# The first expert stage of an image network: experts, norms and q/k/v products of three images in one round

## The reference

```python
t = _to_tokens(x)                                   # per image: 4096 tokens of 128 channels
t = t + _L0_ffn_ref(_ln_t(t), ...)
x = _from_tokens(t, x)
... _L1_conv_ref(_ln_c(x), L1_conv_w_qkv, ...)      # begins with qkv = w_qkv (384 x 128) @ x

# inside _L0_ffn_ref: two of eight experts, the same two for all tokens of an image
h = gelu(einsum('nd,edf->enf', xf, W1) + b1)        # 128 -> 256
y = einsum('enf,efd->end', h, W2) + b2              # 256 -> 128
out = einsum('ne,end->nd', w_dense, y)
out = _layer_norm(out + x, gamma, beta)
```

## Time and profile before

| | |
|---|---|
| median of three runs | 3686.75 us |
| profiled execution | 3690.16 us, its span 3688.4 us |
| TensorE busy over the span | 3175.2 us (86%) |
| VectorE, ScalarE, GpSimd busy | 45%, 41%, 22% |
| mean granted TensorE clock | 0.906 of full speed |
| first expert stage, from its first `up` to its last product | 698.5 to 1476.2 us |

### The profile page before, as it was taken

How to read it: one execution, slowest core, us unless ns; L and a number is a source line. 1 busy time by engine, 2 the same in 40 slices (tenths; PEclk the granted TensorE clock), 3 DMA queues, 4 the chain that set the end, 5 groups by cost and what they waited for, 6 DMA issues and landing times. The chain is left out here.

```text
span 3688.4 us, 66878 instructions
## 1 busy us (share of the span) xinstructions
PE 3175.2 (86%) x27136; PEld 1709.4 (46%) x27136; DVE 1662.3 (45%) x2332; ACT 1520.3 (41%) x2263; POOL 810.5 (22%) x694
## 2 busy tenths in 40 slices
PE   5656675499989997799997779999999999999999
PEld 1146321344445453466665334646364545546444
DVE  5724256465555543111111254545454545545453
ACT  3311253266666664111213344545354444445433
POOL 2410242133333343111110112121211111121221
PEclk7768766699999997899999789999999999999999
DMA  5421464313333323777777321413222231313000
GB/s 187 151 75 23 136 241 207 141 46 137 137 137 137 137 92 143 197 213 215 209 211 250 116 79 46 132 52 103 75 92 91 65 99 54 114 41 126 12 12 24
DMA packets 192537, 438.59 MB, mean 119 GB/s; under 512 B 33340, under 2 KB 100156, under 8 KB 183740
## 3 DMA queue, kind: packets, MB, share of 16 engines
q1 hardware_dynamic: 192356, 436.20, 35.7%
HBM read 247.40 MB, written 188.75 MB: 118 GB/s over the span
## 5 line engine op out<-in xcount | busy, mean ns | idle before, releaser
L2115 DVE TENSOR_TENSOR d_hid_scaled<-d_hid_scaled,d_ps 128x512 f32<-128x512 f32 x512 | 331.1, 684 | 605.3 <-PE d_ps L1802 553.5
L1791 PE MATMUL d_ps<-d_hid_scaled,d_w 128*128 128x512 f32 x1024 | 526.2, 596 | 1.0 <-DVE d_hid_scaled L2115 1.0
L1976 ACT ACTIVATE d_hid_scaled<-d_ps,d_b 128x512 f32<-128x512 f32 x512 | 349.9, 686 | 381.3 <-PE d_ps L1780 368.0
L1519 PE MATMUL c_ps<-c_pad,c_weight 32*32 32x512 f32 x13824 | 474.6, 601 | 27.1 <-ACT c_pad L1471 18.4
L1519 PEld LDWEIGHTS c_ps<-c_pad,c_weight 32*32 32x32 f32 x13824 | 286.7, 103 | 214.5 <-issue 130.5
L1778 PE MATMUL d_ps<-d_tnh,d_w1h 128*128 128x512 f32 x512 | 296.6, 579 | 9.1 <-ACT d_hid_scaled L1976 9.1
L1135 PE MATMUL b_ps<-b_hid,b_w2s 128*128 128x512 f32 x512 | 272.7, 618 | 11.6 <-ACT b_hid L1204 5.8
L1204 ACT ACTIVATE b_hid<-b_ps,b_w1s 128x512 f32<-128x512 f32 x256 | 174.0, 686 | 207.3 <-PE b_ps L1128 205.3
L2063 POOL CAST d_tnh<-d_TN 128x512 fp32r<-128x512 f32 x64 | 39.9, 624 | 972.3 <-PE d_ps L1780 935.0
L1580 DVE COPY c_pad<-c_P 128x1024 f32<-128x1024 f32 x48 | 33.4, 696 | 405.8 <-PE c_ps L1519 380.1
L1791 PEld LDWEIGHTS d_ps<-d_hid_scaled,d_w 128*128 128x128 f32 x1024 | 195.3, 191 | 44.6 <-DVE d_hid_scaled L2115 2.3
(11 more groups left out here) (270 smaller groups left out, 5799.9 us busy)
## 6 DMA issues: line engine op xcount, KB each, us to landing
scratch_qkv<-b_qkv SPq DMA_DIRECT2D x64, 768.0 KB, 3.5
c_P<-scratch_qkv SPq DMA_DIRECT2D x192, 256.0 KB, 4.7
scratch_agg<-c_out SPq DMA_DIRECT2D x192, 256.0 KB, 4.9
d_buf<-scratch_qkv SPq DMA_DIRECT2D x96, 512.0 KB, 4.3
d_buf<-scratch_agg SPq DMA_DIRECT2D x96, 512.0 KB, 3.8
p_X<-in_x SPq DMA_DIRECT2D x8, 2048.0 KB, 7.6
scratch_s<-p_X SPq DMA_DIRECT2D x8, 2048.0 KB, 6.3
m_X<-scratch_s SPq DMA_DIRECT2D x8, 2048.0 KB, 7.8
```

Of the source, the lines that this page charges most:

```text
L1519: end = nc.tensor.matmul(ps[on(i), k * QUADS + h, :].rearrange("p (b r w) -> p b r w", b=2, w=HB), weight[k][on(q), 2 * r + x, on(h)], pad ...
L1791: nc.tensor.matmul(moe_bank, w2[:, e, :], scaled[n % 3][:, :], start=False, stop=(e == E - 1)).then_inc(moe_pe, 1)
L1976: nc.scalar.activation(hid[n % 3][:, :], hid_bank(n), ACT.Gelu, bias=b1[:, n % E:n % E + 1]).then_inc(hid_done, 1)
L2115: nc.vector.tensor_tensor(scaled[n % 3][:, :], hid[n % 3][:, :], spread_bank(n), ALU.mult).then_inc(scaled_done, 1)
```

## The change

Every engine's loop becomes ten rounds of 32 units. In round s stand the experts of image s, the norms of image s - 1 and the products of image s - 2, one product in each of the units 3 to 26. Round 0 has experts alone, round 1 experts and norms, round 8 norms and products, round 9 products alone.

To make room in PSUM the hidden rows keep two banks (3, 4) in place of three, the downs one (6) in place of two, and the products get two of their own (5, 7). So an `up` now waits for the gelu two units back, the first `down` of a chunk waits for the `add` of the chunk before it, and a product waits for the copy two products back.

The first norm's column sums move from ahead of unit 0 to behind unit 2; its root stands at unit 2, its reciprocal at units 3 and 4 (now in two halves of 256 columns), its join at unit 5, its casts at units 6 to 9. The second reciprocal is halved too, at units 24 and 25. The choices go to VectorE's units 1, 2, 11, 12, 13, 15, 17 and 23. On GpSimd the splits, rests and additions get units of their own; on the SyncE queue the stores of three chunks, the image's store, three more chunks, the load of the next normed image, the last two chunks and the load of the next image follow each other.

The core of the diff (the functions' old bodies stand above):

```diff
-        hid_bank = lambda n: banks[3 + n % 3][:, :]
-        y_bank = lambda c: banks[6 + c % 2][:, :]
-        qkv_bank = lambda j: banks[3 + j][:, :]
+        hid_bank = lambda n: banks[3 + n % 2][:, :]
+        y_bank = banks[6][:, :]
+        qkv_bank = lambda m: banks[5 + m % 2 * 2][:, :]
+        QKV = 3
+        product_at = lambda u: divmod(u - QKV, 3) if QKV <= u < QKV + 3 * NCH else None
...
# sync
+                for s in range(1, B + 2):
+                    if s >= 2:
+                        store_qkv(s - 2, range(3))
+                    if s <= B:
+                        store_x2(s - 1)
+                    if s >= 2:
+                        store_qkv(s - 2, range(3, 6))
+                    if 3 <= s + 1 < B:
+                        sp.wait_ge(xl_done, (s - 2) * NCH + NCH)
+                        load_tn(s + 1)
+                    if s >= 2:
+                        store_qkv(s - 2, range(6, NCH))
...
# tensor, in up and down
-                    pe.wait_ge(hid_done, n + 1)
+                    pe.wait_ge(hid_done, n + 2)
...
-                        pe.wait_ge(z_done, b * NCH + c + 1)
+                        pe.wait_ge(z_done, b * NCH + c + 2)
...
+                def norms(b, u):
+                    if u == 2:
+                        norm.variances(pe, 2 * b)
+                    if 6 <= u < 10:
+                        for c in pair(u - 6):
+                            norm.cast_inverse(pe, 2 * b, c, sum_free(b))
...
+                for s in range(B + 2):
                     for u in range(UNITS):
+                        if s < B:
+                            unit(s, u)
+                        if 0 <= s - 1 < B:
+                            norms(s - 1, u)
+                        if s >= 2 and product_at(u):
+                            product(s - 2, *product_at(u))
+                    if s < B:
+                        down(s, UNITS - 2)
+                        down(s, UNITS - 1)
...
# scalar: gelu, then norms, then the square, then copy(s - 2, ...) of the unit
...
# gpsimd
+                        if s < B and 4 <= u < 28 and u % UPS == 0:
+                            split(s, u // UPS + 1)
+                        if s >= 2 and u % 3 == 1 and u < 3 * NCH:
+                            rest(s - 2, u // 3)
+                        if 0 <= s - 1 < B and 8 <= u < 12:
+                            for c in pair(u - 8):
+                                add(s - 1, c)
+                        if s + 1 < B and u in (28, 31):
+                            split(s + 1, (u - 28) // 3)
...
# vector
+                CHOOSE = (1, 2, 11, 12, 13, 15, 17, 23)
...
+                        if s < B and u >= 6 and u % UPS == 2:
+                            add(s, u // UPS - 1)
+                        if 0 <= s - 1 < B:
+                            norms(s - 1, u)
+                        if s >= 2 and u % 3 == 0 and u < 3 * NCH:
+                            high(s - 2, u // 3)
+                        if s + 1 < B and u in CHOOSE:
+                            choose(s + 1, CHOOSE.index(u))
```

More of the change, by code:

```diff
@@ L1208, in sum_squares @@
                     norm.squares(act, 2 * b, c, tn(b), lambda c: act.wait_ge(z_done, b * NCH + c + 3))
[L1210 to L1216, removed]
-                    for u in range(UNITS):
[L1218 to L1245, removed]
@@ new lines, in copy, with norms @@
+                def copy(b, c, j):
+                    m = (b * NCH + c) * 3 + j
+                    if j == 0:
+                        act.wait_ge(qkv_stored[c % 2], (b * (NCH // 2) + c // 2) * 16 + 16)
+                    act.wait_ge(qkv_pe, m + 7)
+                    nc.scalar.activation(qkv[c % 2][:, j, :], qkv_bank(m), ACT.Copy).then_inc(copied, 1)
+                def norms(b, u):
+                    if u < 2:
+                        sum_squares(b, 6 + u)
+                    if u == 2:
+                        norm.deviations(act, 2 * b, eps_t)
+                    if u == 4:
+                        norm.split(act, 2 * b, 1)
+                    if 7 <= u < 11:
+                        for c in pair(u - 7):
+                            norm.wait_out(act, 2 * b, c)
+                            nc.scalar.activation(tn(b)(c), tn(b)(c), ACT.Identity, bias=gb[:, 1:2], scale=gb[:, 0:1]).then_inc(affine_done, 1)
+                    if u == 16:
+                        norm.split(act, b, 0)
+                    if 19 <= u < 23:
+                        for c in pair(u - 19):
+                            norm.squares(act, 2 * b + 1, c, tn(b), lambda c: norm.wait_centred(act, b, c))
+                    if u == 24:
+                        norm.deviations(act, 2 * b + 1, eps_c)
+                    if u == 27:
+                        norm.split(act, 2 * b + 1, 1)
@@ L1247, in _ @@
+                for s in range(B + 2):
+                    for u in range(UNITS):
+                        if s < B:
+                            gelu(s, u)
+                        if 0 <= s - 1 < B:
+                            norms(s - 1, u)
+                        if s < B and 25 <= u < 31:
+                            sum_squares(s, u - 25)
+                        if s >= 2 and product_at(u):
+                            copy(s - 2, *product_at(u))
             @block.gpsimd
@@ L1255, in split, with add @@
                     nc.gpsimd.tensor_tensor(tnl[k][:, :], tn(b)(c), tnh[k][:, :].bitcast(F32), ALU.subtract).then_inc(tnl_done, 1)
-                def add(b, cs):
+                def add(b, c):
                     pool.wait_ge(x_loaded[b % 2], b // 2 * 16 + 16)
[L1259 to L1292, removed]
+                    pool.wait_ge(affine_done, b * NCH + c + 1)
@@ new lines, in add, with rest @@
+                    nc.gpsimd.tensor_tensor(x(b)(c), x(b)(c), tn(b)(c), ALU.add).then_inc(x2_done, 1)
+                def rest(b, c):
+                    pool.wait_ge(xh_done, b * NCH + c + 1)
+                    pool.wait_ge(qkv_pe, (b * NCH + c) * 3 + 3)
+                    nc.gpsimd.tensor_tensor(xl[c % 2][:, :], tn(b)(c), xh[c % 2][:, :].bitcast(F32), ALU.subtract).then_inc(xl_done, 1)
+                split(0, 0)
+                split(0, 1)
+                for s in range(B + 2):
+                    for u in range(UNITS):
+                        if s < B and 4 <= u < 28 and u % UPS == 0:
[7 more added lines that the diff above has]
+                            split(s + 1, (u - 28) // 3)
@@ L1348, in high, with norms @@
                     nc.vector.tensor_copy(xh[c % 2][:, :], tn(b)(c)).then_inc(xh_done, 1)
+                def norms(b, u):
+                    if u == 3 or u == 4:
+                        norm.invert(dve, 2 * b, u - 3)
+                    if u == 5:
+                        norm.join(dve, 2 * b, 1)
+                    if 6 <= u < 10:
+                        for c in pair(u - 6):
+                            norm.scale(dve, 2 * b, c, tn(b), lambda c: dve.wait_ge(z_done, b * NCH + c + 3))
+                    if u == 16:
+                        norm.join(dve, b, 0)
+                    if 18 <= u < 22:
+                        for c in pair(u - 18):
+                            norm.centre(dve, b, c, x(b), tn(b))
+                    if u == 24 or u == 25:
+                        norm.invert(dve, 2 * b + 1, u - 24)
+                    if u == 27:
+                        norm.join(dve, 2 * b + 1, 1)
+                    if 28 <= u < 32:
+                        for c in pair(u - 28):
+                            norm.scale(dve, 2 * b + 1, c, tn(b), lambda c: norm.wait_centred(dve, b, c))
```

114 lines of the change are left out of this document (30 added, 84 removed).

## The result

The changed kernel takes 3699.5 us (3695.4 to 3708.8) against 3692.5 us for the kernel before on the same chips: a ratio of 1.0028, interval 1.0014 to 1.0041. The forecast was 8 us faster; it is 7 us slower, inside the range given and on the wrong side of it. The profiled execution has a span of 3703.2 us.

What follows compares the result with a forecast made beforehand. TensorE, busy 86% of the span, was taken to bound the kernel. Expert rounds gain 17.1 us, the end loses 8.7, total -8.4: from a median of 3686.75 to 3678 us, range 3645 to 3713.

Steps and rivals of the forecast that it cites:

- round 0: Experts alone: 52.5 us plus seven add waits of 0.29 us, 54.5 us.
- rounds 2 to 6: Rounds with products and choices: 80.4 us of work, 10.1 of waits, 2.4 for the clock; 92.9 each, 464.5 together.
- TensorE's own work: A round of experts, norms and 24 products without waits: 80.4 us, unchanged by the edit.
- The waits for the add: TensorE waits for VectorE's add before a chunk's first down; with start and join waits, 10.1 us a round.
- the single bank as the price of the spreading: One bank for the downs: each chunk's first down waits for the previous add, 1.84 us against a unit of 1.56.
- the stall at unit 14: Add behind three experts' choices and one high: 10.7 us against 8.4, a stall of 2.3, with slips 2.6.
- The price of 1.3 us: A VectorE choice instruction beside GpSimd's additions takes 1.30 us start to start, against 0.40 alone.
- The end: Last norms and products: 5.5 us visible, last block 2.7 later and 0.5 longer; +8.7, between 0 and 20.
- The clock: Two waits of 2.6 us per round each bring 3.4 us at half clock; cost 3.4 less 1.0, bounds 0 and 6.8.
- Rival A: Clock stays up and unit 14 is free of GpSimd: about 3645 us with both, 3660 with one; chance 0.35.
- Rival B: Choices meet GpSimd at units 11 to 13, unit 14 stalls 6 us: 3715; chance 0.21 with other slower ways.

Runs made afterwards that it cites:

- Experiments one and two: Changed kernel with each chunk's add one unit earlier on VectorE: 3640.95 us; changed kernel with downs on two banks, products on one: 3630.1 us.
- Experiment six: Changed kernel with the choices at units 0, 1, 2, 14, 15, 19, 20 and 23, away from GpSimd's additions: 3667.6 us, ratio 0.9931.
- experiment eight: Changed kernel with the last image's first two casts to high parts at unit 28 of round 8: 3697.15 us, ratio 1.0016.
- experiment three: Changed kernel with the choices packed at units 9 to 15 and 23, as in the kernel before: 3707.6 us, ratio 1.0041.
- experiment four: Kernel before with only the choices moved to the changed kernel's units: 3663.7 us, ratio 0.9917.

## Why the prediction was wrong

The mechanism was right and some of its sizes were not; since the forecast was a small difference of large terms, -17.1 and +8.7, sizes decided the sign. Measured, they are -4.7 (first `up` to the last image's sums, 703.5 us against 708.1) and +12.5. Term by term from the trace (rounds 0 to 6 end 0.5 us behind the next image's first `up`, where sums would follow the last down; round 7 ends at its sums):

| stretch | forecast | measured |
|---|---|---|
| round 0 | 54.5 | 57.7 |
| round 1 | 83.6 | 84.7 |
| rounds 2 to 6 | 464.5 | 472.4 |
| round 7 | 88.4 | 88.7 |
| round 8 to the first of the last products | 55.1 | 57.7 |
| last products, to the start of the last | 22.3 | 23.5 |

The sum is 16.3 us over the forecast, and half of that is in rounds 2 to 6. TensorE's own work there was right: what is left of a round when the steps lengthened by waits and half clock are put at their undisturbed length is 80.5 to 80.7 us in four of the five, against 80.4.

**The waits for the add** were placed and priced at units 10, 14, 18, 22, 26, 28 and 30 as 1.05, 2.6, 0.65, 1.05, 2.6, 0.5, 1.35 (28 is a join). The trace has 1.19, 3.80, 0.37, 0.77, 2.24, 0.30 and 1.22 of idle time; what the unit takes longer, which is how the forecast worked its stalls out, is some 0.3 more at each, so all but unit 14 are within about 0.4 us of their price. Experiments one and two show that these waits are what the change pays: taken away in either manner, the phase shrinks by 61 and 74 us. The forecast had the single bank as the price of the spreading, and that stands.

**The step that failed most is the stall at unit 14.** It says "I count six of the twelve at 1.3 and six at 0.4, with the high 10.7 us". Measured, from the end of add 1 to the start of add 2 it is 1154.88 to 1167.27, 12.4 us: seven of the twelve are held up, at up to 1.5 us and not 1.3, and the `high`, which I took at 0.4, ran at 1.51. The idle time is 3.80 us and not 2.6, and nearly all half clock of the round follows it (the first pair of downs takes 2.07 us). With its half clock unit 14 costs 5.5 to 7.0 us in rounds 2 to 6, 30.2 in all; the forecast had 2.6 + 2.4, 25.0 in all. That is 5.2 of the 7.9 us. Experiment six takes this wait away and gains 33 us in the phase.

The price of 1.3 us was read from the wrong form. The choices that the earlier trace rows shows beside the additions have one tensor input, the form of the first expert alone; the choices at units 11 to 13 add to what is there, and the trace of the kernel before has such a one beside GpSimd at the higher price:

```profile
1158.29 1.50 DVE L1328 SCALAR_TENSOR_TENSOR b_w1s<-b_w,pick,b_w1s 128x258 f32<-128x258 f32 x1
```

(Also, of the first four choices there three and not four ran at 1.37 to 1.38 us; the first took 0.45.) No term alone turns the sign: with unit 14 as forecast the phase would still be some 2.6 us longer than before.

**Round 0** was too low by 3.2. Its first four units take 8.6 us against 6.9 before (1.7, in the forecast at nothing): the third `up` waits 0.83 us for the first gelu, which stands behind a table load of 1.28 us, where the kernel before had a third hidden bank, and the half clock at the start lasts 8.1 us in place of 5.8. The adds lengthen six units by 0.41 us and one by 0.89, 3.3 in place of 2.0. The rest is the base, 52.7 us in the earlier trace rows and 52.5 in the sum. **The end** was 3.8 too low. The late start of the last block was in the forecast, at 2.7, and experiment eight has it at 2.4. What the products add to round 8 was 5.5 in the forecast and is 57.7 - 46.9 - 2.7 = 8.1 at a clock of 0.77; it was not taken apart further, nor the 1.2 of the last block, and their cause stays open.

**The clock** term (3.4 us at half, twice a round, less an overlap) was near: rounds 2 to 6 have 3.4, 6.8, 3.4, 6.8 and 6.8 us at half clock, but all except one 3.4 stand behind unit 14 and not half of them behind unit 26. Its bounds held. Over the whole phase half clock falls from 92.1 to 71.7 us, worth 10, and the waits take more than that. Rival A's full clock is what the kernels with two banks for the downs and spread choices show in rounds 1 to 7, but it came with the waits' removal, not with the products between the units. Rival B named unit 14 as the place from which it would turn slower, and a third of what the forecast missed came from there (15 us off the forecast in all, and not B's 37). The Trainium skill ("SBUF — State Buffer", "SBUF: two separate sides") calls it an exclusive lock in full, which would bound the held instructions by GpSimd's own; eight held in the changed kernel's round (the high among them) beside eight of GpSimd's, and experiment three, where packing more choices there cost 8 us and not 30, agree with that bound.

**What the change would have been worth.** Its two halves pull apart: spreading the choices alone is 34 us off the phase (experiment four), the whole change 8 us on it. The second bank that the downs gave up costs more than what lies between: taking it back from the products, which need only one while experts run, takes 74 us off and turns the same round structure into 710.7 us.

## What to carry to other kernels

When work is woven in and a buffer is given up for it, ask of each buffer how long its reader has to be late before its writer stalls. Here the products, one per unit, could do with one bank as long as experts run (0.2 to 0.6 us of waits at three of them in a round) and the downs could not, and the opposite was built. On an in-order engine, the instruction that frees a buffer belongs ahead of whatever can wait: one unit earlier was worth 59 us.

A forecast that is the difference of two large terms needs the range and not the sign; compare such kernels by the length of the phase in the trace, since the rest of the program moved by as much as the effect (7.0 of the 14.8 us between the spans).

## What the hardware showed unexpectedly

A choice that adds to its tile takes 0.47 us alone and up to 1.52 beside GpSimd's instructions. VectorE's plain cast from SBUF to SBUF takes 0.43 us alone and 1.51 us beside GpSimd's additions, longer than one addition (5.75 for four here, 5.21 in the earlier trace rows); GpSimd's own were slowed too, by a tenth.

TensorE's clock made the waits dearer in a way that one wait does not tell. A wait of 1.94 us is followed by half clock in some rounds and not in others; the changed kernel's rounds 2 to 6, 9.2 to 9.9 us of waits, show 3.4 or 6.8 us of half clock each; with the early adds, 4.0 us of waits, it is found in rounds 1 to 3 alone of the first eight, with two banks and spread choices, 1.7 us, in none of them (the phase's start left out). With the early adds half clock in the phase fell from 71.7 to 41.0 us, worth 15 of the 61 us gained.
